# Attention and quantised FFN over 16 batches: the last two attention batches and the row work behind them in another order

## The reference

```python
def _ln(t, w, b): ...                      # per head, over 32 features
def _attn(q, k, v):
    s = jnp.einsum('bhqd,bhkd->bhqk', q, k) * SCALE
    p = jax.nn.softmax(s, axis=-1)
    return jnp.einsum('bhqk,bhkd->bhqd', p, v)
q = _ln((x @ Wq + bq).reshape(b, s1, H, HD), qn_w, qn_b)      # 16 heads of 32
k, v = ...                                  # from the first 112 context rows
k_dca, v_dca = ...                          # from the last 16 context rows
ctx = _attn(qT, k, v) + _attn(qT, k_dca, v_dca)
attn = ctx @ Wo + bo

def fake_quant(x, bits, axes):              # round to 127 steps of the row's largest value
...
y = jnp.einsum('bsd,df->bsf', fake_quant(x, 8, -1), fake_quant(kernel, 8, 0))
y = jax.nn.relu(y + fake_quant(bias, 8, -1))
return fake_quant(y, 8, -1)

x = x + attn(_layernorm(x), ctx_1024)
x = x + ffn(_layernorm(x))
```

## Time and profile before

| what | us |
|---|---|
| median of three runs | 372.64 |
| lowest and highest of them | 370.8, 373.56 |
| the profiled execution's own time | 374.78 |
| its span | 373.0 |
| TensorE busy in the span | 324.2 (87%) |
| VectorE busy | 315.6 (85%) |
| ScalarE busy | 224.9 (60%) |
| GpSimd busy | 173.9 (47%) |

### The profile page before, as it was taken

How to read it: one execution, slowest core, us unless ns; L and a number is a source line. 1 busy time by engine, 2 the same in 40 slices (tenths; PEclk the granted TensorE clock), 3 DMA queues, 4 the chain that set the end, 5 groups by cost and what they waited for, 6 DMA issues and landing times.

```text
span 373.0 us, 7598 instructions
## 1 busy us (share of the span) xinstructions
PE 324.2 (87%) x2353; PEld 260.2 (70%) x2353; DVE 315.6 (85%) x804; ACT 224.9 (60%) x444; POOL 173.9 (47%) x261
## 2 busy tenths in 40 slices
PE   1498989799999999999999999999999999868732
PEld 0245657688787878887878787878787877656520
DVE  2987899799989898989898989898989898965664
ACT  3357885365676667676667676767675756542501
POOL 5301512337372828282828282828282827261620
PEclk9999899699999999999999999999999999987985
DMA  7860458418090909090908190919090909090002
GB/s 256 268 262 1 80 123 145 86 38 152 16 174 17 200 29 189 27 189 30 188 19 174 35 207 9 170 45 191 27 194 19 172 2 172 5 172 2 27 2 84
DMA packets 36451, 39.14 MB, mean 105 GB/s; under 512 B 8760, under 2 KB 27452, under 8 KB 36412
## 3 DMA queue, kind: packets, MB, share of 16 engines
q1 hardware_dynamic: 36044, 38.40, 48.6%
q10 hardware_dynamic: 368, 0.27, 0.2%
HBM read 17.15 MB, written 4.72 MB: 59 GB/s over the span
## 4 chain that ended last, share of the span: by engine, by line
PE 65%; issue 5%; DVE 5%; POOL 2%; DMA 2%; ACT 1%; SPq 1%; DVEq 0%; POOLq 0%; ACTq 0%
PE bank L1314 32%; PE bank L1431 12%; PE bank L1400 3%; PE bank L1587 3%; PE bank L1411 3%; PE bank L1412 3%; PE bank L1597 2%; POOL finals L518 1%; PE bank L1489 1%; PE bank L1454 1%; PE bank L1484 1%; DMA k_stack<-k_lo 1%; SPq L370 1%; PE bank L1557 1%; PE bank L1499 1%
## 5 line engine op out<-in xcount | busy, mean ns | idle before, releaser
L1431 PE MATMUL bank<-v_aug,prob_store 128*128 128x66 f32 x512 | 68.7, 278 | 3.8 <-ACT prob_store L732 3.5
L1431 PEld LDWEIGHTS bank<-v_aug,prob_store 128*128 128x128 f32 x512 | 64.4, 195 | 6.4 <-ACT prob_store L732 4.8
L499 POOL TENSOR_TENSOR k_lo<-wkv_raw,k_hi 128x448 f16<-128x448 f32 x16 | 16.8, 1048 | 111.0 <-issue 103.2
L1047 DVE TENSOR_REDUCE neg_max<-bank 128x4 f32<-128x448 f32 (+1 forms) x128 | 45.1, 414 | 7.5 <-PE bank L1400 7.5
L743 ACT ACTIVATE wkv_raw<-bank,affine 128x448 f32<-128x448 f32 (+1 forms) x32 | 22.4, 748 | 42.3 <-PE bank L1484 42.0
L732 ACT ACTIVATE prob_store<-bank,exp_scale 128x512 f32<-128x512 f32 x64 | 41.9, 682 | 7.6 <-PE bank L1412 6.6
L518 POOL TENSOR_TENSOR finals<-seg_out 128x128 f32<-128x128 f32 x64 | 34.5, 547 | 18.8 <-DVE seg_out L1060 18.5
L1411 PE MATMUL bank<-q_stack,k_stack 128*128 128x128 f16 x256 | 33.9, 220 | 1.4 <-ACT maxT L594 1.4
L1412 PE MATMUL bank<-maxT,sel 128*128 128x128 bf16 x256 | 33.7, 219 | 0.0
L1060 DVE TENSOR_TENSOR seg_out<-bank,rden 128x256 f32<-128x256 f32 x64 | 27.2, 424 | 3.8 <-POOL finals L518 1.7
L1411 PEld LDWEIGHTS bank<-q_stack,k_stack 128*128 128x128 f16 x256 | 26.4, 104 | 5.5 <-issue 3.8
(11 more groups left out here) (213 smaller groups left out, 881.1 us busy)
## 6 DMA issues: line engine op xcount, KB each, us to landing
x_in<-in_x SPq DMA_DIRECT2D x16, 256.0 KB, 4.0
q_stack<-q_hi SPq DMA_DIRECT2D x32, 128.0 KB, 3.7
q_stack<-q_lo SPq DMA_DIRECT2D x32, 128.0 KB, 4.8
k_stack<-k_hi SPq DMA_DIRECT2D x32, 128.0 KB, 3.3
k_stack<-k_lo SPq DMA_DIRECT2D x32, 128.0 KB, 4.2
out<-finals SPq DMA_DIRECT2D x16, 256.0 KB, 3.8
y_in<-in_ctx SPq DMA_DIRECT2D x16, 128.0 KB, 3.8
y_dcaT<-in_x SPq DMA_DIRECT2D x8, 256.0 KB, 4.6
```

The costliest lines, as they stand in the source:

```text
L1047: v.tensor_reduce(neg_max[:, HG * gr:HG * (gr + 1), seg], s4[:, :, lo:hi], AX.X, ALU.max, negate=True).then_inc(max_ready.sem, 1)
L1431: last = mm(bank[6 + gr % 2][:, VW * h:VW * (h + 1)], probs[:, gr % 2, h], v_aug[:, Bt.parity, HG * gr + h], start=True, stop=True)
```

## The change

Nothing is added or removed but the place of instructions, in steps 14, 15 and 16:

- Step 14: TensorE transposes the context of 14 before the early scores of 15, and VectorE makes `cT_lo` of 14 before the first maxima of 15. The FFN product of 13 is taken out of this step.
- Step 15: TensorE does the first half of the projection of 14 (six matmuls), then `scores(2)` and `scores(3)` of 15, then the second half. The FFN product of 13 comes behind the transposed maxima. ScalarE scales its rows behind `expo(1)`.
- Step 16: `finish` of 13 and the row maximum of 14 come before `x1` of 15 on VectorE, `finish` of 14 before the FFN result of 15 is scaled, and ScalarE makes the positive part of 14 before it copies `f_intT` of 15.

```diff
@@ ScalarE
+                def scaled_rows(b):
+                    act.wait_ge(*ffn_ready.of(b))
+                    act.wait_ge(*ln2_steps.of(b))
+                    if b.has(1):
+                        act.wait_ge(*yscale_steps.of(b.back(1), 1))
+                    s.activation(f_z, bank[0][:, :], ACT.Copy, scale=f_small[:, 10:11]).then_inc(z_ready.sem, 1)
                 if Bt is not None:
                     expo(0)
                     expo(1)
+                    if final(Bt):
+                        scaled_rows(C.back(1))
...
+                if C is not None and final(C):
+                    positive_rows()
                 if C is not None:
                     act.wait_ge(*fT_ready.of(C))
...
+                if C is not None and not final(C) and (N is None or A is not None):
+                    scaled_rows(C)
@@ VectorE
-                if D is not None and final(D):
-                    finish(D.back(1))
-                if C is not None and not final(C):
+                if C is not None and not final(C) and (Bt is None or not final(Bt)):
                     low_part(cT_lo, cT_hi, bank[6][:, :], chi_ready, attn_ready, C, clo_ready)
...
+                if C is not None and final(C):
+                    finish(D.back(1))
+                    output_maximum()
...
+                if D is not None and (C is None or not final(C)):
+                    output_maximum()
...
+                    if A is None:
+                        low_part(cT_lo, cT_hi, bank[6][:, :], chi_ready, attn_ready, Bt, clo_ready)
                     maxima(0)
                     maxima(1)
                 if C is not None and final(C):
+                    finish(D)
@@ TensorE
+                if Bt is not None and final(Bt):
+                    pe.wait_ge(*chi_ready.of(C))
+                    pe.wait_ge(*clo_ready.of(C))
+                    split_product(bank[7][:, :], cT_hi, cT_lo, wo_hi, wo_lo, range(XC // 2), P)
+                    scores(2)
+                    scores(3)
+                    split_product(bank[7][:, :], cT_hi, cT_lo, wo_hi, wo_lo, range(XC // 2, XC), P
+                                  ).then_inc(attn_ready.sem, 1)
...
                 if Bt is not None and not Bt.first():
                     transposed_maxima()
+                    if final(Bt):
+                        ffn_product(C.back(1))
...
                 if N is not None and A is None:
+                    context()
                     early_scores()
...
+                if C is not None and (N is None or A is not None):
+                    ffn_product(C)
```

83 lines of the change are left out of this document (40 added, 43 removed).

## The result

The changed kernel takes 374.58 us (median of 12 runs, 371.15 to 378.33) against 372.26 us for the kernel before in the same comparison. The ratio is 1.0074 with a 95% interval of 1.0041 to 1.0107. It is slower by about 0.7%, where 372.3 us and a change of -0.3 us were forecast. The ratio leaves out runs over 1.5% above the fastest of their kernel; medians and means here count all runs. Its profiled execution took 375.58 us with a span of 373.8 us, both 0.8 us more than before, and its mean granted clock was 0.951 against 0.961.

The account below looks back on a forecast made before the run. The end was taken as fixed by a chain through all engines, with TensorE's clock low between steps; +1.1 - 0.9 - 0.66 + 0.2 = -0.3 us on 372.64 gave 372.3 us, range 369.5 to 374.5.

Parts of the forecast that it names:

- The early start: Steps 14 and 15: first shifted scores of 15 start at 342.4 instead of 343.90, 1.5 us earlier.
- The new wait on VectorE: Step 15: `bn_stats` of 14 waits for late `z_ready` of 13, so `normalise(0)` starts at 347.55 instead of 346.44, 1.1 us later.
- My sign of being right: Step 15: `normalise(0)` more than 5 us after the first shifted score, where it was 2.54 before.
- everything up to `x1` of 15 comes 1.1 us later: Step 15: the early start is spent, and the lateness of `normalise(0)` carries through to `x1`, +1.1 us.
- low after 341: TensorE's clock: a low clock after 341 would show the forecast wrong.
- Whether the clock returns at the same moment: TensorE's clock in steps 14 and 15: no row tells its return under the new order; it was kept at 340.2.
- the rival that puts a longer low clock there: Low clock lasts through the projection's second half, returning only after 342.4: +1.5 us, 374.1; chance 0.17.
- Step 16, -0.9 and -0.66: Row maximum of 14 leaves the chain of 15, -0.9 us; `finish` of 14 moves into the FFN wait, -0.66 us.
- `finish` of 13 beside GpSimd's scaling, +0.2: Step 16: collision with GpSimd's scaling of 14 delays `x1` of 15 from 357.59 to 357.8, +0.2 us.
- The level: Whole kernel: the -0.3 us was put on the median of the three runs shown, 372.64, giving 372.3 us.
- the gap of step 14: TensorE's 2.91 us wait: the clock fell at 333.4 before the context could start, so no clock saving was expected.

Follow-up runs that it names:

- e18: Kernel before in its own order plus spare matmuls in three waits: four behind step 14's transposed maxima, twelve before early scores of 15, eighteen in the last; mean 369.26 us.
- e15: e12 plus four spare matmuls before the context of 14; mean 366.35 us, ratio 0.9786 to 0.9894 against the kernel before.
- e9: Kernel before with one move: ScalarE scales the FFN rows of 13 behind `expo(1)` of 15; mean 374.47 us.
- e1: Only the step 16 part of the change, steps 14 and 15 as in the kernel before; mean 370.86 us.
- e2: Only the step 14 and 15 parts of the change, step 16 as in the kernel before; mean 376.19 us.
- e4: Changed kernel, statistics of 14 not waiting for `z_ready`, row maximum of 13 behind `normalise(1)`, GpSimd centring and rounding 14 before scaling 13; mean 374.85 us.
- e5: Changed kernel with the FFN rows of 13 scaled by one VectorE instruction between `x1` and `bn_stats` of 14; mean 371.57 us.
- e6: Changed kernel plus spare matmuls, five before `weigh(2)` of 15 and five before the transposed integers of 14; mean 374.12 us.
- e10: Changed kernel with ScalarE's scaling of 13 before `expo(0)` of 15 instead of behind `expo(1)`; mean 372.26 us.
- e13: Changed kernel plus eighteen spare matmuls in the last wait, before the last transposed integers; mean 371.52 us.
- e14: Changed kernel plus the spare matmuls of both e13 and e6; mean 371.57 us.
- e11: Changed kernel plus the spare matmuls of e14 and four before the context of 14; mean 371.59 us.
- e16: Changed kernel with the early scores of 15 put back in front of the context of 14; mean 375.03 us.
- e3: Changed kernel with the FFN product of 13 back in step 14 behind the early scores, its scaling behind the copy to `cT_hi`; mean 370.92 us.
- e7: Kernel before plus twelve spare matmuls before the early scores of 15, in the 2.91 us wait for the transfer; mean 370.77 us.
- e12: e8 plus eighteen spare matmuls behind the projection of 15, in the last wait; mean 369.38 us.
- e17: e15 plus four more spare matmuls behind the transposed maxima of step 14; mean 367.18 us.
- e8: e3 with the projection of 14 whole behind `scores(2)` and `scores(3)` instead of in halves; mean 369.92 us.

## Why the prediction was wrong

- **The early start, -1.5 us: right at the full clock, not shown otherwise.** It was 1.24 us in the profile and 1.53 us between e18 and e15. That the clock returned at 340.3 against a forecast of 340.2 is luck: this low stretch had begun at 323.2, that of before at 333.4. And the old order's length was read from one execution. From the end of the last combine of 14 to the first shifted score of 15 the old order took 10.21 us in the profile of before, 9.04 in e9 and 6.54 in e1, with 6.5, 3.4 and 0.5 us of low clock in it. The changed kernel took 8.98, and e2, e4, e5, e6, e10, e13 and e14, with TensorE's order of step 14 unchanged from it and no spare matmuls there, 8.44 to 9.44. The means don't show the early start either: e2 should lie 1.5 us below e9 and lies 1.7 us (1.2) above it.
- **The new wait on VectorE: right in place and mechanism.** `normalise(0)` came at 347.53 against a forecast of 347.55, and the mean of e9 (+2.64, 0.66) is near the 2.6 us charged for it. My sign of being right, `normalise(0)` more than 5 us after the first shifted score, was just missed (4.87). e4 adds what I didn't have: the signal's lateness also loads GpSimd, so that to free VectorE alone gives nothing.
- **The step that failed is the clock in the terms of steps 14 and 15. In the profiled pair it is the price of the new wait, the sentence that "everything up to `x1` of 15 comes 1.1 us later".** It carried the lateness of `normalise(0)` on at the old durations, that is at full clock: 16.5 us from shifted scores to `x1`. With spare matmuls in the two waits the stretch takes 15.92 to 15.94 us (e6, e11, e14), so at full clock the late scaling costs 2.2 us over the 13.69 of before, even less than my 2.8 (which has the +0.2 of `finish` in it). Without them it takes 16.68 to 17.41 us (the changed kernel, e2, e4, e9, e13, e16). I knew of a wait of 1.06 us on ScalarE and of `weigh(2)` being late, but did not ask what TensorE does in that time. It stood for 1.39 and 1.35 us, its clock fell at 350.5 ("low after 341" was one of my signs of being wrong), and `weigh(3)`, the FFN product of 14 and the first matmuls of the projection of 15 ran at half speed. In all six profiles with a late scaling and unfilled waits the clock is low for 3.4 to 6.8 us between 344 and 358 (in e4 the wait is the one for the combines), in none of the three with filled waits. The waits are not the only way to it: of the others before, e3, e7, e12, e15, e17 and e18 have none there, but e1, e5, e8 and e10 have 2.1 to 6.8 us. In the profile of the changed kernel the low clock is worth 17.22 - 15.94 = 1.3 us, more than the forecast's whole difference to what came (+0.8 against -0.3). The means don't confirm this 1.3 us, as said at e6 and e14.
- **In the means it is the clock of the run, priced at nothing.** "Whether the clock returns at the same moment ... no row tells. Here I keep 340.2" held for that moment, and the rival that puts a longer low clock there did not happen. But on average a run of the changed kernel has 7.8 us (1.9) more low clock than before, by the fit 1.8 us of the 2.95 between -0.3 and +2.65. I had looked for it in one gap only. Where the 7.8 us arise stays open: filling both new waits took away 6.1 us (3.3) from e13 to e14 but no time, and 2.0 us (2.8) from the changed kernel to e6. The order of context and early scores has no part in it (e16); that of the projection and the product may have. e15 has four spare matmuls in front of the context and 10.4 us (4) less low clock than e12, while the same ones between e14 and e11 change nothing (17.7 and 17.5 us). One profile of a kernel doesn't show its usual low clock either. By windows of 2 us the profile of before has 10.2 us of low clock ahead of 320, where both kernels are the same, and that of the changed one 3.4; from 320 to 344 they have 6.8 and 17.0, and e2, with the same TensorE order as the changed kernel, has 3.4. In 8 of the 20 profiles a low stretch begins at 321 to 326, ahead of everything that moved. It holds about 17 us in the changed kernel, e5, e13, e14 and e16, 14 in e3 and e8 (product of 13 in step 14) and 10 in e1 (the old order). So its start isn't due to the order; whether the new order makes it last longer was not tested.
- **Step 16, -0.9 and -0.66: right.** 13.92 us against a forecast of 13.85 from `x1` on; e1 alone gives -1.34 at equal low clock (-0.97, 0.67, by the means).
- **`finish` of 13 beside GpSimd's scaling, +0.2: it came to nothing.** The collision was there, with roles changed:

```profile
356.94 1.78 POOL L528 TENSOR_TENSOR wq_raw<-wq_raw,fk_scale 128x512 f32<-128x512 f32 x1 [1.96 <-ACT wq_raw L810]
```

VectorE was first (356.82, 0.75 us), and GpSimd took 1.78 us instead of the 1.29 of the earlier trace rows. The row maximum waited 1.18 us for it and ended just as the last matmul of the projection did, at 359.8, so `x1` lost nothing by it. In e3 (these rows) and e15 it was the other way about:

```profile
353.21 1.29 POOL L528 TENSOR_TENSOR wq_raw<-wq_raw,fk_scale 128x512 f32<-128x512 f32 x1 [1.71 <-ACT wq_raw L810]
...
353.34 1.71 DVE L1046 SCALAR_TENSOR_TENSOR finals<-wo_raw,f_small,fk_raw 128x512 f32<-128x512 f32 x1 [0.27 <-DMA out<-finals]
```

From the first matmul of the projection to `x1` it took 3.11 us in e3 and 3.08 before. The Trainium skill (SBUF — State Buffer, "Who interferes with whom") says that a VectorE instruction with two SBUF inputs contends with a GpSimd instruction that reads SBUF, and that their shared port pair is an exclusive lock. The traces nearly agree: the one that began second took 0.5 us longer (GpSimd) and 0.96 us longer (VectorE), and ended 0.14 to 0.20 us sooner than if it had run in full behind the first; the first ran at its usual length.
- **The level.** The forecast was put on a median of three runs, 372.64. That of all runs is 371.83 as a mean, so -0.3 us meant a ratio of 0.999; measured was 1.0074.

The Trainium skill (TensorE: Matmul & The Clock Gate, "HAM oscillation — how this bites in real kernels") advises, for thin matmuls, a loop order that keeps TensorE from idling through transfer waits. The prediction said of the gap of step 14 that nothing would be saved there, and for the moved context that held: the clock fell before it. Spare matmuls in that gap did help: in the profile of e7 the clock is full from 320 to 344, and its mean is 1.1 us (0.6) below before. With the last wait filled too (e18) it is 2.6 us (0.5), and from `x1` to the end 14.36 us instead of 15.41. So the traces agree with the advice.

## What to carry to other kernels

When a producer is moved behind work of another batch, follow its signal through every engine that takes its queue in order, and then ask what TensorE does meanwhile: a wait costs a second time where the clock falls at it (1.3 us in the profile here). A saving that rests on one long gap in one execution should be read in a second one first: the gap of 2.91 us was gone in e1, where the clock had fallen earlier. Before reordering the end of a pipeline, fill its known waits with spare matmuls and measure again. At a steady clock the early start and the end came out within 0.1 us of a sum made from one timeline; at an unsteady one a change of 1.5 us is lost in its scatter.
